# One-hot sort and eight queue-issued runs in place of indirect scatters, in a graph layer followed by a routed feed-forward layer

## The chip, the cores and the metric

One core of one Trainium2 chip runs the whole kernel. The metric is device time in microseconds (us) of one launch.

## The reference

For N = 12500 nodes with 256 features, 212500 edges sorted by destination, and 8 experts:

```python
# x: (12500, 256)   src, dst, edge_weight: (212500,)
msgs = layernorm(x)[src] * edge_weight[:, None]
x = x + (segment_sum(msgs, dst, 12500) @ W.T + b)          # graph layer
n = layernorm(x)
probs = softmax(n @ gate_w + gate_b)                       # 8 experts
top2_vals, top2_idx = top_k(probs, 2)
for e in range(8):                                         # routed layer
    w_e = top2_vals where top2_idx == e, else 0
    x = x + w_e[:, None] * (gelu(n @ W1[e] + b1[e]) @ W2[e] + b2[e])
```

## The kernel before

**Edges.** The edges stand in 208 groups of 1024. POOL fetches a group with 8 indirect gathers of 128 rows of 1 KB (L363). VectorE builds eight 128x80 spread matrices (L975), TensorE sums the group with 8 matmuls (L599), ScalarE copies the sums out (L782), TensorE turns them (L589) and VectorE adds them into a ring of node columns (L988). Three buffers of rows stand between POOL and TensorE.

**Nodes.** There are 98 tiles of 128 nodes. When a tile's groups are in, TensorE does the linear layer (L619), VectorE adds it to x and works out the layer norm (L1009 to L1025, `node`), ScalarE writes the normalised rows into `xs` (L788), and TensorE turns them (L630) and takes the gate's logits (L639). SP stores x1 (L475), which waits for VectorE's sum.

**Routing.** The tiles form 17 parts (6, then mostly 8, at the end 4 and 2 tiles). For a part, VectorE does the softmax, `choose` (the two largest, L1053 to L1073) and `place` (the row of each choice in its expert's queue, L1084 to L1141, with the list of items), with a count by TensorE between them (`rank`, L647 and L648). Then POOL sends each tile to the queues in DRAM with two indirect scatters of 128 rows of 1088 bytes (`send`, L391), one for the first choices and one for the second.

**Items.** 128 rows of one expert's queue are an item; there are 231. SP loads an item with an address read from a list (`load_xi`, L492 and L493). TensorE turns it (L655), multiplies by W1 (L667), turns the result (L676) after ScalarE's copy (L811), multiplies by W2 (L685) after ScalarE's gelu (L822). VectorE adds the bias and scales (L1152 to L1156), and POOL scatters the result rows (L396). VectorE's next but one item waits for that scatter to land. At the end of an epoch SP writes blank rows behind the eight queues (`fill_tails`, L480 and L481). Finally each node tile's two results are fetched and added to x1 (L504, L505, L1163, L1165) and stored (L510).

**Order.** All engines walk one list of turns that `plan` writes before the build. Turn t holds the gather of group t (POOL), the matmuls of group t-1, the turning of group t-2, at most one node tile, and one or two pipeline steps of items: in a step one item is at gelu and W2, the next at W1, a third is turned, and a fourth is loaded. So an item that SP loads in a turn with one step is turned by TensorE in the following turn. In 208 turns with gathers there is one step, or two in every other turn while over 6 items wait; after them come three steps a turn. Inside a turn TensorE's matmuls of the group come behind the first step, and a second step behind those. Each engine takes its instructions strictly in the order written; SP's order in a turn is:

```python
if t.load_x >= 0: load_x(t.load_x)
for step in t.steps:
    if step[3] >= 0: load_xi(step[3])
for u in t.combines: store_out(u)
for u in t.fetches: load_results(u, u in EPOCH_TILES)
if t.linear >= 0: store_x1(t.linear)
```

Of the kernel before, what the change touches and what calls it, by code (L numbers as in the profile page):

```python
# [35 lines left out]
RING = 16  # L36
# [23 lines left out]
NI = FIRST_ITEM[-1]  # L60
XI = 6
# [46 lines left out]
class Turn:  # L108
# [11 lines left out]
    sends: list = field(default_factory=list)  # L120
# [6 lines left out]
def plan(with_sums):  # L127
# [7 lines left out]
    while True:  # L135
# [87 lines left out]
def build(nc, x, src, dst, wgt_in, first, last, gnn_wT_in, gnn_b, gate_w, gate_b, w1_in, b1_in, w2_in, b2, out):  # L223
# [6 lines left out]
    xhat = nc.dram_tensor("xhat", (N, D), F32, kind="Internal").ap()  # L230
    blocks = slots.rearrange("(n p) f -> n p f", p=P)
    x_main, xhat_main = (a[0:P * LJ].rearrange("(p j) f -> p j f", p=P) for a in (x, xhat))
    with ExitStack() as s:
# [13 lines left out]
        iota_w, part_iota, valid = sb("iota_w", [P, W]), sb("part_iota", [P, 1]), sb("valid", [P, 1])  # L247
# [29 lines left out]
        top, top_r, slot_f = sb("top", [P, NTM]), sb("top_r", [P, NTM]), sb("slot_f", [P, NTM, 2])  # L277
        slot_i = sb("slot_i", [P, NT, 2], I32)
# [33 lines left out]
        sent, blank_out, tails_in = sems("sent", NK), sem("blank_out"), sem("tails_in")  # L312
# [26 lines left out]

        def wait_sent(eng, k):  # L340
            eng.wait_ge(sent[k], 32 * SIZES[k])
# [11 lines left out]
        def _(pool):  # L353
# [27 lines left out]
            nc.gpsimd.iota(block_f[0][:], pattern=[[BLOCKS, NX]], base=0, channel_multiplier=0, allow_small_or_imprecise_dtypes=True)  # L381
            nc.gpsimd.iota(item_iota[:], pattern=[[1, NI]], base=0, channel_multiplier=0,
# [3 lines left out]

            def send(t):
                k, n = PART_OF[t], valid_rows(t)
                pool.wait_ge(routed, k + 1)
                for c in range(2):  # L390
                    pool.indirect_dma_start(slots, bass.IndirectOffsetOnAxis(ap=slot_i[0:n, t, c:c + 1], axis=0),  # L391
                                            xs[0:n, t % XR, :], None).then_inc(sent[k], 16)
# [6 lines left out]
            def turns(plan, fast):  # L399
                for t in plan:  # L400
                    if t.gather >= 2:
                        if t.gather >= R:
                            pool.wait_ge(summed, t.gather - R + 1)
                        if t.gather == RAW:
                            wait_xhat()
                        gather(t.gather)
                    for u in t.sends:
                        send(u)
                    for i in t.results:
                        scatter_result(i)  # L410
# [17 lines left out]
        def _(sp):  # L428
# [41 lines left out]
            sp.wait_ge(blank_out, 16 * NX)  # L470
# [5 lines left out]

            def fill_tails(k):
                sp.wait_ge(routed, k + 1)
# [4 lines left out]
            def load_xi(i):  # L483
                k = part_of_item(i)
                if i == 0 or part_of_item(i - 1) != k:
                    sp.wait_ge(listed, k + 1)
                    wait_sent(sp, k)
# [34 lines left out]
            def turns(plan, fast):  # L522
                for t in plan:
                    if t.prep >= 0:
                        load_ahead(t.prep + 4)
                    if t.refill >= 0:
                        refill(t.refill)
                    if t.load_x >= 0:
# [12 lines left out]
                    if t.place >= 0 and ends_epoch(t.place):  # L541
                        fill_tails(t.place)
# [37 lines left out]
        def _(pe):  # L580
# [26 lines left out]
            def linear(t, fast):  # L607
# [8 lines left out]
                else:  # L616
                    pe.wait_ge(x1_ready, t)
                for k in range(KD):
                    done = nc.tensor.matmul(B_NODE[:, 0:D], tile(t)[:, k, :], gnn_wT[:, k, :], start=k == 0, stop=k == KD - 1)  # L619
                done.then_inc(lin_summed, 1)  # L620

# [79 lines left out]
            def turns(plan, fast):  # L701
                for t in plan:
                    for a, b, _, _ in t.steps[:1]:
                        step_up(a, b)
                    if t.add >= 0:
                        turn_sums(t.add)
                    if t.gate >= 0:
                        turn_node(t.gate)
                    if t.linear >= 0:
# [30 lines left out]
        def _(act):  # L740
# [43 lines left out]
            def normalise(t):  # L784
                if t >= XR:
                    wait_sent(act, PART_OF[t - XR])
                act.wait_ge(coef_ready, t + 1)
                nc.scalar.activation(xs[:, t % XR, 0:D], x_t[t % XB][:], ACT.Identity,  # L788
                                     bias=shift[t % XB][:], scale=rstd[t % XB][:]).then_inc(xn_ready, 1)

# [41 lines left out]
            def turns(plan, fast):  # L832
                for t in plan:
# [4 lines left out]
                    if t.prep >= 0:  # L838
                        block_root(t.prep)
                        normalise_rows(t.prep)  # L840
                    for a, b, _, _ in t.steps[:1]:
                        step_up(a, b)
                    if t.gate >= 0:
                        copy_xnT(t.gate)
                    for _, _, c, _ in t.steps[:1]:
                        if c >= 0:
                            copy_xiT(c)
                    if t.softmax >= 0:
# [23 lines left out]
        def _(dve):  # L872
            nc.vector.memset(eps[:], EPS)
            nc.vector.memset(acc[:], 0.0)
            nc.vector.memset(item_f[:], 0.0)
            for a in got + res:
# [35 lines left out]
            nc.vector.tensor_scalar(valid[:], part_iota[:], float(LAST), None, op0=ALU.is_lt)  # L912
            for n in keep_et:
                nc.vector.memset(keep_et[n][:, 0::n], 0.0)
            first_then(nc.vector.scalar_tensor_tensor(blank[:, C_ID:], id_base[:, 0:NX], float(2 * NPAD), blank[:, C_ID:],
                                                      op0=ALU.add, op1=ALU.add))
            nc.vector.memset(empty[:, 0:C_ID], 0.0)
# [158 lines left out]
            def place(k):  # L1076
# [10 lines left out]
                then(nc.vector.tensor_tensor(upto, upto, counts, op=ALU.subtract))  # L1087
                then(nc.vector.tensor_tensor(ps, by_expert(upto).rearrange("p e t -> p t e"), per_expert(end_old, n), op=ALU.add))
                nc.vector.tensor_tensor(ps, ps, B_GATE[:, 0:n * NX].rearrange("p (t e) -> p t e", e=NX), op=ALU.add).then_inc(gate_free, 1)
# [190 lines left out]
```

## Time and profile before

| | |
|---|---|
| time, median of 3 runs | 2976.65 us (2972.73 to 2977.03) |
| time of the profiled execution | 2972.42 us |
| its span, first to last instruction | 2970.7 us |
| granted TensorE clock, mean | 0.867 of full speed |
| busy: TensorE / VectorE / ScalarE / POOL | 74% / 47% / 25% / 68% |
| mean busy share of the 16 DMA engines | about 0.5, 146 GB/s |

SP does no arithmetic and has no row in the busy shares; what it does is read from the timeline of its queue. POOL's share counts only the body of each indirect DMA; the time between two of them is called "issue". In the rows, PE is TensorE, PEld its weight loads, DVE is VectorE, ACT is ScalarE, and SPq is SP's queue. A row's "<-" in brackets names what ended the idle time before it.

### The profile page before, as it was taken

How to read it: one execution, taken by the hardware profiler on the slowest of the kernel's cores; microseconds unless marked ns; L12 is line 12 of the kernel's file. 1: busy time of each engine (PE TensorE's matmuls, PEld its weight loads, DVE VectorE, ACT ScalarE, POOL GpSimd, SP SyncE). 2: the span in 40 equal slices, each digit the busy share in tenths (PEclk: the TensorE clock that was granted, in tenths of full speed). 3: DMA queues.
4: the chain of work that ended last, by engine and by line, in shares of the span. 5: the costliest groups of instructions: out<-in, count | busy, mean ns of one | idle time of the engine just before them, and what ended most of it. 6: DMA issues, size and time to landing. Idle time of an engine off the chain costs nothing.

```text
span 2970.7 us, 40845 instructions
## 1 busy us (share of the span) xinstructions
PE 2187.7 (74%) x9206; PEld 1475.6 (50%) x9207; DVE 1407.6 (47%) x5982; ACT 739.1 (25%) x1985; POOL 2011.7 (68%) x2107
## 2 busy tenths in 40 slices
PE   3555765785785978975966877977877887878655
PEld 2333543553563655653644654655555555545433
DVE  8756344344354444454463453453555455454342
ACT  3311110221221322220321221322222222224322
POOL 6547777777777777777777777777777777761211
PEclk9668877988898998987987987988998899889878
DMA  9563433443444443455555544434455565542352
GB/s 339 200 232 115 124 117 114 137 124 114 134 128 136 134 125 120 132 148 173 165 166 161 148 138 127 136 119 124 136 163 161 167 188 154 159 125 90 107 159 81
DMA packets 231445, 432.24 MB, mean 146 GB/s; under 512 B 47020, under 2 KB 158542, under 8 KB 228006
## 3 DMA queue, kind: packets, MB, share of 16 engines
q0 software_dynamic: 100368, 275.72, 31.2%
q1 hardware_dynamic: 128246, 144.38, 15.4%
q10 hardware_dynamic: 2592, 9.45, 0.8%
q8 instruction: 90, 1.47, 0.2%
q14 instruction: 149, 1.22, 0.1%
HBM read 326.80 MB, written 102.56 MB: 145 GB/s over the span
## 4 chain that ended last, share of the span: by engine, by line
POOL 51%; issue 19%; PE 14%; DVE 10%; DMA 3%; ACT 1%; ACTq 1%; DVEq 0%; SPq 0%; POOLq 0%
POOL rows L363 41%; POOL slots L391 5%; POOL results L396 5%; PE bank L599 5%; PE bank L685 4%; PE bank L667 3%; DVE spread L975 1%; DMA results<-y_sb,result_i 1%; PE bank L676 1%; DMA got<-results 1%; DVE item_t L1123 1%; DVE y_sb L1153 1%; DVE pre_bn L931 1%; DVE square_n L1022 0%; DVE bn L954 0%
## 5 line engine op out<-in xcount | busy, mean ns | idle before, releaser
L363 POOL DMA_INDIRECT rows<-xhat,src_t x1536 | 1469.2, 956 | 476.2 <-issue 464.7
L599 PE MATMUL bank<-rows,spread 128*80 128x256 f32 x3328 | 915.4, 437 | 317.1 <-issue 150.0
L599 PEld LDWEIGHTS bank<-rows,spread 128*80 128x80 f32 x3328 | 566.5, 176 | 603.9 <-issue 314.9
L685 PE MATMUL bank<-w,hT 128*128 x1848 | 482.6, 407 | 97.1 <-ACT hT L822 52.7
L685 PEld LDWEIGHTS bank<-w,hT 128*128 128x128 f32 x1848 | 361.4, 202 | 207.4 <-issue 160.9
L667 PE MATMUL bank<-w,xiT 128*128 x924 | 447.7, 607 | 12.5 <-ACT xiT L805 2.8
L988 DVE TENSOR_TENSOR acc<-acc,bank 128x160 f32 x208 | 67.0, 322 | 775.4 <-PE bank L589 753.0
L396 POOL DMA_INDIRECT results<-y_sb,result_i x231 | 227.2, 984 | 242.4 <-DVE y_sb L1156 186.3
L975 DVE TENSOR_SCALAR spread<-iota_w,dst_rel,wgt 128x80 f32<-128x80 f32 x1536 | 378.8, 342 | 0.2
L1152 DVE CAST result_i<-xi 128x1 int32 x231 | 35.5, 154 | 612.5 <-PE bank L685 327.8
L822 ACT ACTIVATE hT<-bank,b1T 128x128 f32<-128x128 f32 x924 | 263.3, 367 | 215.4 <-PE bank L676 209.6
L391 POOL DMA_INDIRECT slots<-xs,slot_i x196 | 190.7, 973 | 113.1 <-issue 79.0
L782 ACT ACTIVATE sums_n<-bank 80x256 f32<-80x256 f32 x192 | 71.2, 371 | 679.7 <-PE bank L599 679.7
L805 ACT ACTIVATE xiT<-bank 128x256 f32<-128x256 f32 x231 | 88.6, 383 | 579.5 <-PE bank L655 579.5
L667 PEld LDWEIGHTS bank<-w,xiT 128*128 128x128 f32 x924 | 159.4, 192 | 144.3 <-issue 143.7
L363 POOL DMA_INDIRECT rows<-in_x,src_t x128 | 122.3, 956 | 100.4 <-PE bank L603 60.4
L811 ACT ACTIVATE h_sb<-bank 128x512 f32<-128x512 f32 x231 | 138.7, 601 | 122.1 <-PE bank L667 122.0
L589 PEld LDWEIGHTS bank<-ident,sums_n 80*128 80x128 f32 x416 | 51.9, 144 | 224.9 <-ACT sums_n L782 138.7
L589 PE MATMUL bank<-ident,sums_n 80*128 80x80 f32 x416 | 69.8, 250 | 117.4 <-ACT sums_n L782 89.9
L788 ACT ACTIVATE xs<-x_t,shift,rstd 128x256 f32<-128x256 f32 x98 | 58.3, 595 | 351.7 <-DVE shift L1025 351.7
L676 PE MATMUL bank<-ident,h_sb 128*128 128x128 f32 x924 | 140.4, 275 | 1.9 <-ACT h_sb L811 1.9
L676 PEld LDWEIGHTS bank<-ident,h_sb 128*128 128x128 f32 x924 | 114.1, 143 | 23.8 <-ACT h_sb L811 2.8
(159 smaller groups left out, 1750.4 us busy)
## 6 DMA issues: line engine op xcount, KB each, us to landing
xi<-slots SPq DMA_DIRECT2D x231, 136.0 KB, 2.8
got<-results SPq DMA_DIRECT2D x97, 256.0 KB
rows<-xhat,src_t POOLq DMA_INDIRECT x1536
x_t<-in_x SPq DMA_DIRECT2D x97, 128.0 KB
x_d<-x_t SPq DMA_DIRECT2D x97, 128.0 KB, 2.4
res<-x_d SPq DMA_DIRECT2D x97, 128.0 KB
out_nodes<-res SPq DMA_DIRECT2D x97, 128.0 KB
w<-in_x SPq DMA_DIRECT2D x12, 1024.0 KB, 12.7
```

Source lines behind the costliest of these rows:

```text
L363: pool.indirect_dma_start(rows[q][:, c, :], None, x if g < RAW else xhat, bass.IndirectOffsetOnAxis(ap=src_t[:, g * CG + c:g * CG + c + 1] ...
L391: pool.indirect_dma_start(slots, bass.IndirectOffsetOnAxis(ap=slot_i[0:n, t, c:c + 1], axis=0), xs[0:n, t % XR, :], None).then_inc(sent[k] ...
L396: pool.indirect_dma_start(results, bass.IndirectOffsetOnAxis(ap=result_i[i % 2][:], axis=0), y_sb[i % 2][:], None).then_inc(y_out[i % 2], 16)
L589: done = nc.tensor.transpose(B_TURN[:, k * W:(k + 1) * W], sums_n[:, k * P:(k + 1) * P], ident[0:W, 0:W])
L599: done = nc.tensor.matmul(B_SUM[0:W, 0:D], spread[g % 2][:, c, :], rows[q][:, c, :], start=c == 0, stop=c == CG - 1)
L667: done = nc.tensor.matmul(B_H[:], xiT[i % 2][:, b, :], w1[:, bass.ds(e, 1), b, :].rearrange("p o h -> p (o h)"), start=b == 0, stop=b == K ...
L676: done = nc.tensor.transpose(B_HT[:, j * P:(j + 1) * P], h_sb[i % 2][:, j * P:(j + 1) * P], ident[:])
L685: done = nc.tensor.matmul(B_Y[:, 0:D], hT[i % 2][:, j, :], w2[:, bass.ds(e, 1), j, :].rearrange("p o f -> p (o f)"), start=j == 0, stop=j ...
L805: nc.scalar.activation(xiT[i % 2][:].rearrange("p k n -> p (k n)"), B_XI[:, 0:D], ACT.Copy).then_inc(xiT_ready, 1)
L811: nc.scalar.activation(h_sb[i % 2][:], B_H[:], ACT.Copy).then_inc(h_ready, 1)
L822: done = nc.scalar.activation(hT[i % 2][:, j, :], B_HT[:, j * P:(j + 1) * P], ACT.Gelu, bias=b1T[:, bass.ds(e * KH + j, 1)])
L975: done = nc.vector.tensor_scalar(spread[g % 2][:, c, :], iota_w[:], dst_rel[:, g * CG + c:g * CG + c + 1], w8[:, c:c + 1] if g < RAW else ...
```

## The change

POOL's `send` goes. In its place, one tile in each turn from the turn of its part's `place` on passes through four turns:

- `mask_choices` (VectorE, end of the turn): two 128x256 comparisons make a one-hot matrix. Its column is the place of a choice among the tile's 256 choices sorted by expert.
- `sort` (TensorE, next turn): two matmuls of that matrix with the tile's rows of `xs` (272 columns); ScalarE copies each result (`copy_sorted`). The bank is the one that `linear` uses, so `linear`, which now stands behind the first step, waits for the second copy.
- `store_sorted` (SP, the turn after): one store of the 256 sorted rows to one of three stage buffers in DRAM.
- `copy_runs` (SP, one turn later): for each of the 8 experts SP reads two registers (where the run starts in the stage, where it goes in the queue) and issues one DRAM to DRAM DMA of 128 rows. What lies behind the run's end is overwritten by the next tile's run, so each tile waits for all eight copies of the tile before.

`place` gets six more small instructions. The items of a part open only when the copies of its last tile have been issued, one tile a turn (before: two). After the last gather there is now one step a turn (before: three) until the last tile's copies are issued. The ring of node columns falls from 16 tiles to 8. In SP's turn the new work stands ahead of the loads of items:

```diff
@@ plan
-        for _ in range(2 if busy else 4):
-            if send_next < NT and place_at.get(PART_OF[send_next], tau) < tau:
-                t.sends.append(send_next)
-                if send_next == PARTS[PART_OF[send_next]][1] - 1:
-                    sent_at[PART_OF[send_next]] = tau
-                send_next += 1
+        if turns:
+            t.sort, t.stage, t.runs = turns[-1].mask, turns[-1].sort, turns[-1].stage
+        if send_next < NT and place_at.get(PART_OF[send_next], tau + 1) <= tau:
+            t.mask = send_next
+            send_next += 1
+        if t.runs >= 0 and t.runs == PARTS[PART_OF[t.runs]][1] - 1:
+            sent_at[PART_OF[t.runs]] = tau
-        n_steps = (1 + (waiting > 6 and tau % 2 == 0)) if busy else 3
+        n_steps = (1 + (waiting > 6 and tau % 2 == 0)) if busy else 1 if NK - 1 not in sent_at else 3
@@ SP
+            def store_sorted(t):
+                if t >= STAGES:
+                    sp.wait_ge(runs_in, 16 * NX * (t - STAGES + 1))
+                sp.wait_ge(sorted_ready, 2 * t + 2)
+                sp.dma_start(stages[t % STAGES][0:2 * P].rearrange("(h p) f -> p h f", p=P), sorted_x[t % 2][:]).then_inc(staged[t % STAGES], 16)
+            def copy_runs(t):
+                k = PART_OF[t]
+                j = (t - PARTS[k][0]) * NX
+                sp.wait_ge(routed, k + 1)
+                sp.wait_ge(staged[t % STAGES], 16 * (t // STAGES + 1))
+                if t:
+                    sp.wait_ge(runs_in, 16 * NX * t)
+                if t in EPOCH_TILES[1:]:
+                    sp.wait_ge(tails_in, 16 * NX * EPOCH_OF[k])
+                for e in range(NX):
+                    a = sp.value_load(run_from[k % 2][:, j + e:j + e + 1], min_val=0, max_val=2 * P)
+                    b = sp.value_load(run_to[k % 2][:, j + e:j + e + 1], min_val=0, max_val=NX * S - 2 * P)
+                    sp.dma_start(slots[bass.ds(b, P), :], stages[t % STAGES][bass.ds(a, P), :]).then_inc(runs_in, 16)
@@ SP turns
                     if t.refill >= 0:
                         refill(t.refill)
+                    if t.stage >= 0:
+                        store_sorted(t.stage)
+                    if t.runs >= 0:
+                        copy_runs(t.runs)
                     if t.load_x >= 0:
                         load_x(t.load_x)
@@ TensorE
                     if t.add >= 0:
                         turn_sums(t.add)
+                    if t.sort >= 0:
+                        sort(t.sort, 0)
                     if t.gate >= 0:
                         turn_node(t.gate)
+                    for a, _, c, _ in t.steps[:1]:
+                        step_down(a, c)
+                    if t.sort >= 0:
+                        sort(t.sort, 1)
                     if t.linear >= 0:
                         linear(t.linear, fast)
-                    for a, _, c, _ in t.steps[:1]:
-                        step_down(a, c)
@@ VectorE
+            def mask_choices(t):
+                nc.vector.tensor_scalar(first_choice[:], iota_s[:], at[0], None, op0=ALU.is_equal).then_inc(half_mask, 1)
+                nc.vector.scalar_tensor_tensor(sort_mask[t % 2][:], iota_s[:], at[1], first_choice[:],
+                                               op0=ALU.is_equal, op1=ALU.add).then_inc(mask_set, 1)
```

## Rows read from the trace of the kernel before

**Rows 1.** The page's chain that ended last, by engine and line.

```profile
POOL 51%; issue 19%; PE 14%; DVE 10%; DMA 3%; ACT 1%; ACTq 1%; DVEq 0%; SPq 0%; POOLq 0%
```

**Rows 2.** Busy time by engine from 256 to 2676 us, with instruction counts.

```profile
256.00:2676.00 2420.00, 1851.41 (x7781) 1250.00 (x7781) 1126.91 (x4755) 571.00 (x1550) 1813.37 (x1886) 0.88 0.47 140
```

**Rows 3.** Timeline of POOL at 1283 us: start, duration.

```profile
1285.04 0.97 POOL L363 DMA_INDIRECT rows<-xhat,src_t  x1 [0.30 <-issue]
...
1295.07 0.99 POOL L396 DMA_INDIRECT results<-y_sb,result_i  x1 [0.30 <-issue]
```

**Rows 4.** Timeline of TensorE: group sums that bound the long stage.

```profile
250.85 5.34 PE L599 MATMUL bank<-rows,spread 128*80 128x256 f32 x16 [1.14 <-issue]
...
1062.61 3.65 PE L599 MATMUL bank<-rows,spread 128*80 128x256 f32 x16
...
1285.26 3.68 PE L599 MATMUL bank<-rows,spread 128*80 128x256 f32 x16 [0.73 <-DMA rows<-xhat,src_t]
...
2670.26 5.79 PE L599 MATMUL bank<-rows,spread 128*80 128x256 f32 x16
...
2680.77 3.65 PE L599 MATMUL bank<-rows,spread 128*80 128x256 f32 x16 [0.34 <-issue]
```

**Rows 5.** Timeline of TensorE: first instructions of two turns, and of the second's extra step.

```profile
1219.63 0.60 PE L676 MATMUL bank<-ident,h_sb 128*128 128x128 f32 x4
...
1229.15 0.60 PE L676 MATMUL bank<-ident,h_sb 128*128 128x128 f32 x4
...
1233.25 0.60 PE L676 MATMUL bank<-ident,h_sb 128*128 128x128 f32 x4
```

**Rows 6.** Waits between 1066 and 1289 us: total us, times, longest.

```profile
DVE result_i L1152 <- DMA results<-y_sb,result_i: 29.2, 6, 9.1
```

**Rows 7.** Waits between 500 and 2600 us: total us, times, longest.

```profile
PEld bank L599 <- DMA rows<-xhat,src_t: 112.1, 24, 10.0
...
PEld bank L647 <- DVE both L1067: 84.1, 12, 12.7
```

**Rows 8.** SP's instructions for a blank store with an address: duration ns min/median/max.

```profile
L480 SPq TENSOR_LOAD <-end_i x40: 263/273/524, 893.3 to 2841.9; - x40
L480 SPq FUSED_REGOPS  x40: 147/147/154, 893.6 to 2842.2; - x40
L480 SPq SEQ_ASSERT  x40: 18/18/18, 893.7 to 2842.4; - x40
...
L481 SPq FUSED_REGOPS  x40: 42/42/42, 893.8 to 2842.5; - x40
L481 SPq MOVE slots<-blank x40: 29/29/37, 893.9 to 2842.6; - x40
L481 SPq DMA_DIRECT2D slots<-blank x40: 332/332/761, 894.0 to 2842.6; - x40
```

**Rows 9.** Timeline of SP's queue at 2834 us.

```profile
2834.73 8.21 SPq L481 DMA_DIRECT2D slots<-blank  x8
```

**Rows 10.** Timeline of SP's queue at 1501 us.

```profile
1502.87 0.43 SPq L510 DMA_DIRECT2D out_nodes<-res  x1
1503.40 0.37 SPq L504 DMA_DIRECT2D res<-x_d  x1
1503.82 0.48 SPq L505 DMA_DIRECT2D got<-results  x1
```

**Rows 11.** DMA issues by line: KB each, median us to landing.

```profile
xi<-slots SPq DMA_DIRECT2D x231, 136.0 KB, 2.8
...
slots<-blank SPq DMA_DIRECT2D x40, 136.0 KB, 2.5
```

**Rows 12.** Groups by line: busy us, mean ns of one.

```profile
L805 ACT ACTIVATE xiT<-bank 128x256 f32<-128x256 f32 x231 | 88.6, 383 | 579.5 <-PE bank L655 579.5
```

**Rows 13.** Timeline of TensorE in the tail: two items' first steps, and the last item.

```profile
2861.80 0.60 PE L676 MATMUL bank<-ident,h_sb 128*128 128x128 f32 x4
...
2866.28 0.60 PE L676 MATMUL bank<-ident,h_sb 128*128 128x128 f32 x4
...
2939.91 1.99 PE L685 MATMUL bank<-w,hT 128*128 x8 [1.41 <-ACT hT L822]
```

**Rows 14.** The page's DMA queues: packets, MB, share of 16 engines.

```profile
q0 software_dynamic: 100368, 275.72, 31.2%
q1 hardware_dynamic: 128246, 144.38, 15.4%
```

More of the change, by code:

```diff
@@ L35 @@
 NPAD = NT * P
-RING = 16
+RING = 8
 RCOLS = RING * P
@@ L60 @@
 NI = FIRST_ITEM[-1]
+STAGE = 3 * P
+STAGES = 3
 XI = 6
@@ L119 @@
     refill: int = -1
-    sends: list = field(default_factory=list)
+    mask: int = -1
+    sort: int = -1
+    stage: int = -1
+    runs: int = -1
     steps: list = field(default_factory=list)
@@ L230, in build @@
     xhat = nc.dram_tensor("xhat", (N, D), F32, kind="Internal").ap()
+    stages = [nc.dram_tensor(f"stage{i}", (STAGE, XW), F32, kind="Internal").ap() for i in range(STAGES)]
     blocks = slots.rearrange("(n p) f -> n p f", p=P)
@@ L469, in _ @@
                 sp.dma_start(blocks[(e + 1) * BLOCKS - 1], empty[:]).then_inc(blank_out, 16)
-            sp.wait_ge(blank_out, 16 * NX)
+            for a in stages:
+                sp.dma_start(a[2 * P:], blank[:]).then_inc(blank_out, 16)
+            sp.wait_ge(blank_out, 16 * (NX + STAGES))
             def store_x1(t):
@@ L527, in turns @@
                         refill(t.refill)
+                    if t.stage >= 0:
+                        store_sorted(t.stage)
+                    if t.runs >= 0:
+                        copy_runs(t.runs)
+                        k = PART_OF[t.runs]
+                        if t.runs == PARTS[k][1] - 1 and ends_epoch(k):
+                            fill_tails(k)
                     if t.load_x >= 0:
@@ L620, in linear, with sort @@
                 done.then_inc(lin_summed, 1)
+            def sort(t, h):
+                if h == 0:
+                    pe.wait_ge(mask_set, t + 1)
+                pe.wait_ge(x1_ready, n_linear[0])
+                if t or h:
+                    pe.wait_ge(sorted_ready, 2 * t + h)
+                nc.tensor.matmul(B_NODE[:, 0:XW], sort_mask[t % 2][:, h * P:(h + 1) * P], xs[:, t % XR, :],
+                                 start=True, stop=True).then_inc(sort_done, 1)
+            n_linear, n_sorted = [0], [0]
             def turn_node(t):
@@ L847, in turns @@
                             copy_xiT(c)
+                    if t.sort >= 0:
+                        copy_sorted(t.sort, 1)
                     if t.softmax >= 0:
@@ L875, in _ @@
             nc.vector.memset(item_f[:], 0.0)
+            nc.vector.memset(xs[:], 0.0)
+            nc.vector.memset(keep_te[:], 1.0)
             for a in got + res:
@@ L916, in _ @@
                                                       op0=ALU.add, op1=ALU.add))
+            nc.vector.memset(keep_te[:, 0::NX], 0.0)
             nc.vector.memset(empty[:, 0:C_ID], 0.0)
@@ L1096, in place @@
                         dve.wait_ge(tails_in, 16 * NX * EPOCH_OF[k])
-                    nc.vector.tensor_copy(end_i[:], end[0:1, :])
-                nc.vector.tensor_copy(slot_i[:, t0:t1, :], slot_f[:, 0:n, :]).then_inc(routed, 1)
+                    then(nc.vector.tensor_copy(end_i[:], end[0:1, :]))
+                dve.sem_inc(routed, 1)
                 if ends_epoch(k):
-                    dve.wait_ge(routed, k + 1)
                     then(nc.vector.tensor_scalar(round_i[:], end[:], float(P - 1), None, op0=ALU.add))
@@ L1104, in place @@
                 list_items(k, end)
+            def mask_choices(t):
+                k = PART_OF[t]
+                j = t - PARTS[k][0]
+                at = [place_f[k % 2][:, c, j:j + 1] for c in range(2)]
+                if t:
+                    dve.wait_ge(mask_set, t)
+                if t >= 2:
+                    dve.wait_ge(sort_done, 2 * (t - 2) + 2)
+                nc.vector.tensor_scalar(first_choice[:], iota_s[:], at[0], None, op0=ALU.is_equal).then_inc(half_mask, 1)
+                dve.wait_ge(half_mask, t + 1)
+                nc.vector.scalar_tensor_tensor(sort_mask[t % 2][:], iota_s[:], at[1], first_choice[:],
+                                               op0=ALU.is_equal, op1=ALU.add).then_inc(mask_set, 1)
             def list_items(k, end):
```

68 lines of the change are left out of this document (46 added, 22 removed).

## The prediction

> **What bounds the kernel now.** I read the page's chain first: POOL's indirect DMAs and the issue time between them are 70% of it [rows 1]. The busy table of the long stage, 256 to 2676 us, says how full POOL is: 1886 instructions in 2420 us [rows 2], one each 1.28 us, while POOL's timeline has them 10.03 us / 8 = 1.254 us apart when nothing is waited for [rows 3]. So POOL is 98% full there. The page's 68% hides this, since it leaves out the 0.30 us before each.
>
> The second thing is how near TensorE is. From the end of group 16's sums (256.2) to that of group 206 (2676.1) there are 190 turns of 12.74 us [rows 4]. In POOL's own terms: 1520 gathers, 184 scatters of tiles and 188 of results, by the planner's rules, 1892 x 1.254 = 2373 us. TensorE waited for rows only 112 us in 2100 [rows 7]. One part of 17 turns, groups 85 to 101, took 1288.9 - 1066.3 = 222.7 us [rows 4], of which 29.2 us were VectorE waiting for POOL's result scatters [rows 6]. Without POOL it would have been 193.5 us, 11.4 a turn. This is what TensorE's chain adds up to: 17 x 9.5 us for a turn with one step, 6 x 4.1 us for second steps [rows 5], and 84.1 / 12 = 7.0 us in the turn of `choose`, where the count and then the group's sums stand behind VectorE [rows 7]: 193.1 us. So TensorE's chain is only 1.3 us a turn below POOL.
>
> SP is the engine to look at, since the work goes there. It is idle most of a turn, but strictly in order, and an item that it loads in one turn is turned in the next.
>
> **The change, part by part.**
>
> *POOL.* 184 scatters go in the long stage and 6 result scatters move past it: 190 x 1.254 = 238 us. POOL then needs 1702 x 1.254 = 2134 us, 11.2 a turn. This is the most that the long stage can gain, and only if all else keeps that pace.
>
> *TensorE, ScalarE, VectorE.* A sort is two matmuls of 272 columns. Eight of 256 columns take 3.65 us [rows 4], so 2 x 0.46 x 1.06 = 0.97 us, and where `linear` follows it waits for ScalarE's second copy, 0.38 us [rows 12] and a hand-over: 1.4 us a tile. It can't be below nothing, and if both copies are waited for it is some 2. `linear` behind the first step moves the node's norm, `choose` and the count later by a W2 product and a turn, 1.9 + 0.4 = 2.3 us, in 14 turns. The masks (two comparisons of 256 columns, some 0.9 us) and `place`'s six instructions (some 1.3 us) lie in VectorE's idle half, and in the rest between `place` and the next spread. If that cover is gone they cost 8 x 0.9 + 1.3 us a part.
>
> *SP.* This decides. A blank store with one address from a register has a period of (8.21 - 0.33) / 7 = 1.13 us [rows 9]. Its pieces are the load, its range arithmetic and assertion, 0.273 + 0.147 + 0.018 = 0.44 us, the address, 0.07 us, and the DMA, 0.33 us, with some 0.05 us between any two of the six [rows 8]. No row shows a DMA with two addresses from registers. From below: the second costs nothing, 1.13 us. From above: a second load with its gaps, 0.58, a second address, 0.17, and the slowest DMA issue seen, 0.76 for 0.33 [rows 8]: 2.3 us. I take 1.13 + 0.58 + 0.17 = 1.88, rounded to 1.85 us, since the second load is the same work as the first. Eight are 14.8 us a tile.
> The Trainium skill (DMA: Bandwidth & Descriptors, Latency and other measured facts) gives a floor of about 600 ns for a tensor load. The row has 0.27 us. By the page's figure a run would be an estimated 2.5 us, a tile 20, and the kernel near 3600 us; the row decides.
>
> The rest of SP's turn with runs: the store of the sorted rows 0.5, 63 items over 90 such turns at 1.13, 0.8; x and x1, 0.4; results in 32 of them at some 1.45 [rows 10], 0.5; semaphore waits 0.2. That is 2.4, and 17.2 us together, against TensorE's 11 to 12.
>
> Who waits: behind the copies in SP's queue stands the load of the item that TensorE turns in the next turn. At the first turn with copies SP has most of a turn in hand; from the second on TensorE gets its item at SP's pace, 17.2 us a turn, and with TensorE wait the group's sums, and so POOL's rows. By the planner's rules 90 turns of the 190 have copies, in 14 bursts (6, seven of 8, then 8, 6, 4, 4, 4 and two of the last 4). 90 - 14 = 76 turns go at SP's pace: 76 x 17.2 = 1307 us. In 23 of the 90 no item is loaded, and SP can be a turn further behind before two full buffers of sorted rows stop ScalarE: back 50 us.
>
> The other 114 turns go at TensorE's pace, since POOL has three buffers in hand after a burst: 102 x 9.5, 12 without a step x 5.4, 38 second steps x 4.1, 14 x (7.0 + 2.3) for `choose`, 42 sorts x 1.4: 969 + 65 + 156 + 130 + 59 = 1379 us. POOL needs 1280 for them.
>
> The long stage: 1307 - 50 + 1379 = 2636 for 2420 us, +216.
>
> *Tail.* Before, it is 2970.7 - 2684.4 = 286 us [rows 4]. After: turns 209 to 222 hold 7 turns with copies at some 18 us (two fetches of results each), less 4 x 6 in hand, and 7 at some 8 us, 158 us. Then items 197 to 230, 34 x 4.48 us [rows 13], 152, less 13 that lie in turn 222, and as before 29 us from the last product to the end [rows 13]: 326, +40 us. The idle stretch of the old tail is filled, but by slow turns. Start (a memset, three more blanks) and twelve folds for six: +8 us.
>
> Sum, on the profiled execution's own 2972.4 us, which is 4.2 below the median of the runs and is kept as the base: 2972.4 + 216 + 40 + 8 = 3236; I say 3240 us.
>
> **The rivals.**
>
> *The copies are cheap or hidden: faster.* If a run cost 1.13 us, SP's turn would be 11.5 us and never late. TensorE's chain would then bound, 193.5 + 8 x 1.4 + 2.3 = 207 us a part, 12.2 a turn: -105 us, with a tail of some 280: about 2865 us, and by POOL alone 2690. For it: DMA issue alone is 0.33 of the 1.13 us [rows 8]. Against it: the rest is there each time, and now twice. It decides from SP turns of 13.7 us down, a run of 1.4 us.
> The Trainium skill (Perfetto Trace Analysis, What "DMA-bound" means) names solid DMA slices on the issuing engine's track as the sign that the issuer binds, and large descriptors as the help. By that rule alone the eight large copies are 3 us of slices and this rival holds; the register loads between the slices are not in it.
>
> *Part of it is hidden.* Runs of 1.45 to 1.65 us, or SP further ahead at each burst than I think: 2985 to 3130 us.
>
> *The copies themselves are slow.* A tile now moves 8 x 128 rows from DRAM to DRAM. At the SP queue's mean of 0.154 x 16 x 2970.7 / 128246 = 57 ns a packet that is 3.7 us of all 16 DMA engines, at the indirect queue's 148 ns it is 9.5 us [rows 14], with some 8 us a turn of other traffic [rows 2]. Landing is 2.5 to 2.8 us for such a size [rows 11], and each tile waits for the eight before, issued last some 2.5 us earlier: little or no wait. If they land in 6 us, each turn grows by 3.5: 76 x 3.5 = 266, some 3500 us.
>
> *No change*: needs the gain on POOL and the loss on SP to meet within 6 us.
>
> **How the numbers follow.** SP's pace as costed, 3130 to 3360 us: 0.60. Slow copies or issue, above that: 0.10. Part hidden: 0.11. Within 0.2% (about what a measurement of this kernel can tell from no change): 0.03. Faster: 0.16. Slower is 0.60 + 0.10 + 0.11 = 0.81. The range is 2985 to 3440 us: it leaves out the faster and the equal case and the far end of the slow ones, some 2 in 10.
>
> **What would show it.** SP's queue in a burst: rows of eight copies some 1.85 us apart, and hardly idle. TensorE in those turns waits for the load of xi, 5 us a turn, which today costs it next to nothing. POOL is no longer full: it waits for the sums of a group. Turns are 17 us in bursts and 10 to 13 between. It would be wrong if the copies stand 1.4 us apart or less, if POOL's issues stay 1.25 us apart through the stage, or if TensorE's waits for xi stay small.

## The result, and the profile after

The changed kernel takes 3613.71 us (3610.18 to 3620.73), beside 2976.84 us for the kernel before on the same chip: ratio 1.215, interval 1.2134 to 1.2165, 637 us more. The forecast was 3240 us with a range of 2985 to 3440: the direction was right, the loss was 2.4 times the one forecast. The profiled execution took 3620.73 us (span 3619.0, mean clock 0.82), and the rows of after are from it.

The chain, by engine and by line, to be set against [rows 1]:

```profile
SPq 36%; PE 25%; DVE 15%; issue 13%; DMA 7%; ACT 1%; ACTq 1%; POOL 0%; DVEq 0%; POOLq 0%
SPq L501 13%; SPq L500 10%; SPq L499 10%; PE bank L630 8%; PE bank L712 6%; PE bank L730 6%; DMA slots<-stage 4%; DVE spread L1041 2%; PE bank L721 1%; DMA xi<-slots 1%; PE bank L662 1%; DVE item_t L1214 1%; PE bank L700 1%; DVE square_n L1088 1%; DMA got<-results 1%
```

In the chain, SP had 0% and has 36% now. 33% are three lines: the two register loads (L499, L500) and the copy (L501). POOL fell from 51% to 0%.

Busy time of the long stage, which now runs from 239 to 3212 us ([rows 2]):

```profile
239.00:3212.00 2973.00, 1971.86 (x8042) 1333.97 (x8043) 1201.13 (x4989) 636.89 (x1699) 1630.87 (x1696) 0.82 0.50 147
```

POOL has 190 instructions fewer, as costed, but the stage is 553 us longer. The DMA share is 0.50 beside 0.47: on the mean the transfers don't fill the 16 DMA engines. TensorE's granted clock fell from 0.88 to 0.82 in this stage, where it waits more. That isn't where the time went: without the sort's matmuls (L662, 142 us) TensorE was busy for 1830 us, beside 1851 before, with six items fewer in the stage.

SP's queue in a burst (start, duration; [rows 9, 10]):

```profile
310.34 14.53 SPq L501 DMA_DIRECT2D slots<-stage  x8
324.96 0.52 SPq L466 DMA_DIRECT2D x_t<-in_x  x1
325.57 0.38 SPq L486 DMA_DIRECT2D stage<-sorted_x  x1
329.28 14.48 SPq L501 DMA_DIRECT2D slots<-stage  x8
```

From one block of eight copies to the next it is 18.94 us here, in a turn that loads no item and no results. The pieces of a run are in the instruction rows ([rows 8]; duration ns min/median/max):

```profile
L499 SPq TENSOR_LOAD <-run_from x784: 262/271/901, 290.6 to 3430.7; - x196
L499 SPq FUSED_REGOPS  x784: 147/147/159, 291.1 to 3431.3; - x196
L499 SPq SEQ_ASSERT  x784: 18/18/31, 291.3 to 3431.5; - x196
```

```profile
L501 SPq MOVE slots<-stage x1568: 29/29/43, 292.2 to 3432.3; - x196
L501 SPq FUSED_REGOPS  x784: 60/60/66, 292.1 to 3432.2; - x196
L501 SPq DMA_DIRECT2D slots<-stage x784: 525/531/717, 292.4 to 3432.4; - x196
```

The load and its arithmetic cost what the blank store's did, and come twice. The issue of a DRAM to DRAM copy with two register addresses takes 0.531 us where the blank store's took 0.332.

Waits over the whole run (total us, times, longest; [rows 7]):

```profile
PE bank L700 <- DMA xi<-slots: 622.9, 62, 42.5
```

```profile
POOL rows L374 <- PE bank L630: 506.8, 63, 35.8
```

```profile
SPq L495 <- DMA slots<-stage: 34.2, 32, 2.0
```

TensorE waits for the load of an item, and POOL for TensorE. SP stands idle for the copies' landing (L495 is `copy_runs`' wait) for 34 us in all. The chain's 4% for the landing are more, some 145 us, since the chain counts the whole time from the issue of a block's last copy to its landing; in most of that time SP issues other transfers, and only the rest is idle. One such piece of the chain, beside the SP rows above (start, duration):

```profile
324.33 3.07 DMA slots<-stage
```

SP issued until 325.95 and then idled until 327.41. Two rows of TensorE's timeline show that bursts in which no item is loaded are late too:

```profile
330.12 1.25 PE L662 MATMUL bank<-xs,sort_mask 128*128 128x272 f32 x2 [9.87 <-ACT sorted_x L846]
...
403.26 0.69 PE L700 MATMUL bank<-ident,xi 128*128 128x128 f32 x2 [42.54 <-DMA xi<-slots]
```

In the first the sort waits for ScalarE, whose two buffers of sorted rows wait for SP's store. In the second the first item behind a burst pays SP's whole lag at once.

### The profile page after: what moved, and what is told of

Same layout as the page of the kernel before. It is cut to its first block, busy times and chain, and to the rows that moved or that the text cites. A ratio compares the mean times of both kernels' runs of the same rounds, so it can differ in the third digit from the quotient of the medians.

```text
span 3619.0 us, 50501 instructions
## 1 busy us (share of the span) xinstructions
PE 2351.8 (65%) x9598; PEld 1586.3 (44%) x9599; DVE 1495.4 (41%) x6264; ACT 822.3 (23%) x2181; POOL 1823.7 (50%) x1912
## 3 DMA queue, kind: packets, MB, share of 16 engines
q8 instruction: 94, 1.54, 0.2%
## 4 chain that ended last, share of the span: by engine, by line
SPq 36%; PE 25%; DVE 15%; issue 13%; DMA 7%; ACT 1%; ACTq 1%; POOL 0%; DVEq 0%; POOLq 0%
SPq L501 13%; SPq L500 10%; SPq L499 10%; PE bank L630 8%; PE bank L712 6%; PE bank L730 6%; DMA slots<-stage 4%; DVE spread L1041 2%; PE bank L721 1%; DMA xi<-slots 1%; PE bank L662 1%; DVE item_t L1214 1%; PE bank L700 1%; DVE square_n L1088 1%; DMA got<-results 1%
## 5 line engine op out<-in xcount | busy, mean ns | idle before, releaser
L700 PE MATMUL bank<-ident,xi 128*128 128x128 f32 x462 | 106.1, 317 | 622.9 <-DMA xi<-slots 622.9
L712 PE MATMUL bank<-w,xiT 128*128 x924 | 474.6, 639 | 10.4 <-ACT xiT L862 2.2
L700 PEld LDWEIGHTS bank<-ident,xi 128*128 128x128 f32 x462 | 66.4, 159 | 667.6 <-DMA xi<-slots 648.0
L662 PE MATMUL bank<-xs,sort_mask 128*128 128x272 f32 x392 | 151.2, 472 | 202.9 <-DVE sort_mask L1194 161.7
L712 PEld LDWEIGHTS bank<-w,xiT 128*128 128x128 f32 x924 | 168.3, 203 | 152.3 <-issue 151.0
L662 PEld LDWEIGHTS bank<-xs,sort_mask 128*128 128x128 f32 x392 | 70.1, 221 | 215.1 <-DVE sort_mask L1194 167.6
```

The costliest lines, as they stand in the source:

```text
L662: nc.tensor.matmul(B_NODE[:, 0:XW], sort_mask[t % 2][:, h * P:(h + 1) * P], xs[:, t % XR, :], start=True, stop=True).then_inc(sort_done, 1)
L700: done = nc.tensor.transpose(B_XI[:, b * P:(b + 1) * P], xi[i % XI][:, b * P:(b + 1) * P], ident[:])
L712: done = nc.tensor.matmul(B_H[:], xiT[i % 2][:, b, :], w1[:, bass.ds(e, 1), b, :].rearrange("p o h -> p (o h)"), start=b == 0, stop=b == K ...
```

## The experiments

Eighteen runs were made. Twelve had chips where the kernel before took 2973 to 2978 us. Six (e5 to e8, e17, e18) had chips where it took 3706 and 3713 us; their ratios stand only beside each other. The microseconds of the two kinds are not compared. The edits are shown shortened. In the expectations, theory A is that SP's instructions set the pace, theory B that it is the sort, the masks, the order or the tail plan, theory C that it is the copies' transfers or their landing.

| run | us | over the kernel before on its chip | ratio, interval |
|---|---|---|---|
| e1_pool_scatters | 3137.94 | +165 | 1.055 (1.0519 to 1.0581) |
| e2_third_load | 4066.56 | +1094 | 1.3672 (1.3630 to 1.3714) |
| e3_double_bytes | 3723.45 | +750 | 1.2518 (1.2482 to 1.2555) |
| e4_items_first | 3653.65 | +681 | 1.2284 (1.2248 to 1.2319) |
| e9_changed_again | 3625.86 | +651 | 1.2176 (1.2146 to 1.2206) |
| e10_one_load | 3276.77 | +302 | 1.1009 (1.0975 to 1.1043) |
| e11_spread | 3124.79 | +150 | 1.0507 (1.0490 to 1.0525) |
| e12_combined | 2964.05 | -11 | 0.9963 (0.9950 to 0.9976) |
| e13_spread_mask_first | 3109.66 | +132 | 1.0455 (1.0435 to 1.0476) |
| e14_spread_one_load | 3002.03 | +24 | 1.0087 (1.0071 to 1.0104) |
| e15_tail_three_steps | 3619.86 | +642 | 1.2162 (1.2133 to 1.2191) |
| e16_scatters_mask_first | 3150.32 | +172 | 1.0587 (1.0569 to 1.0605) |
| e5, one load | 4188.22 | +483 | 1.1295 (1.1262 to 1.1329) |
| e6, spread | 4158.49 | +453 | 1.1210 (1.1164 to 1.1255) |
| e7 and e18, split | 4310.95, 4325.39 | +605, +612 | 1.1640, 1.1604 |
| e8, combined | 3884.99 | +179 | 1.0499 (1.0464 to 1.0534) |
| e17_copies_last | 4472.13 | +759 | 1.2030 (1.1991 to 1.2069) |

**e1: without the copies.** Masks, sort, stage store and order stay; POOL sends each tile by two scatters in place of SP's copies.

```diff
-                        copy_runs(t.runs)          # SP
+                        send(t.runs)               # POOL, two indirect scatters
```

> The changed kernel with its plan, masks, sort, ScalarE copies and store of the sorted rows, but the rows go to the queues by POOL's two indirect scatters a tile in the turn where SP copied the runs; SP's copies are gone (the sorted rows are stored and not used; place has some five more small instructions). Theory A (SP's in-order copies, 19 us a tile, are what is lost): near the kernel before plus the sort and the later items, 2980 to 3080 us. Theory B (the sort on TensorE, the masks behind place, the later linear and the tail plan are what is lost): 3300 us or more. Theory C (the traffic from DRAM to DRAM): as A.

3138 us: SP's copies in place of POOL's scatters are 476 of the 637 us. (That is the exchange of the two, since POOL has its scatters back in this run; `place` has some five more small instructions.) The other 165 (stage 2563 for 2420 us, tail 327 for 286, start 17 us sooner) belong to sort, masks, `place`, the smaller ring of node columns and the new order; the ring was in no run changed by itself. TensorE's waits for the loads of items, 623 us in the changed kernel, are gone with the copies:

```profile
PE bank L694 <- DMA xi<-slots: 4.3, 2, 3.7
```

**e2: one register load more per run.**

```diff
                     b = sp.value_load(run_to[k % 2][:, j + e:j + e + 1], ...)
+                    sp.value_load(run_to[k % 2][:, j + e:j + e + 1], ...)
```

> The changed kernel with one more register load per run, whose value is not used: 8 x 0.56 = 4.5 us more of SP a tile. Theory A: every tile's copies lie on the path, so 98 x 4.5 = 440 us more, about 4050 us. Theory B: SP is not what sets the pace, under 60 us more. Theory C (the copies' transfers set the pace): the loads lie beside them, under 100 us more.

+453 us, 98 x 4.6: a run's pace is 2.480 us for 1.915. A register load with its arithmetic, 0.565 us on SP, moves no byte of the payload and costs its full length, in every tile.

**e3: twice the rows in each copy.** Nothing is left out; the rows beyond a run are overwritten as before.

```diff
-                    sp.dma_start(slots[bass.ds(b, P), :], stages[t % STAGES][bass.ds(a, P), :])
+                    sp.dma_start(slots[bass.ds(b, 2 * P), :], stages[t % STAGES][bass.ds(a, 2 * P), :])
```

> The changed kernel with copies of 256 rows for 128 (stages of 512 rows): twice the bytes from DRAM to DRAM, the same number of instructions on SP. Theory A: no change to speak of, 3600 to 3660 us. Theory C (transfer or landing of the copies sets the pace): 200 us more at least. Theory B: no change.

+110 us for 109 MB more. A run's pace stays (1.913 us for 1.915); SP's wait for the landing grew:

```profile
SPq L496 <- DMA slots<-stage: 127.7, 68, 4.2
```

That is 94 us more, most of the 110. So the transfers have a price, a small one at the changed kernel's size.

**e4: all of SP's new work behind the item, x and result loads.**

```diff
+                    [load_x, load_xi, store_out, load_results]
                     if t.stage >= 0:
                         store_sorted(t.stage)
                     if t.runs >= 0:
                         copy_runs(t.runs)
-                    [load_x, load_xi, store_out, load_results]
```

> The changed kernel with the store of sorted rows and the copies moved behind the loads of items, x and results in SP's turn. Theory A: the item that TensorE waits for is loaded some 16 us earlier, but SP still needs 19 us a tile, so each of the 14 long bursts gains at most one block: 14 x 16 = 220 us less, 3370 to 3450 us. Theory B and C: under 60 us.

A miss: 40 us slower instead of 160 to 240 faster. The items' loads stand in front, and TensorE waits for them nearly as long as before (593 us for 623); the stage's store went back with the copies, and ScalarE now waits for it, for 246 us, where it was 40:

```profile
PE bank L700 <- DMA xi<-slots: 593.2, 51, 53.6
```

```profile
ACT sorted_x L846 <- DMA stage<-sorted_x: 246.0, 35, 15.9
```

So SP is short of time, and not only badly ordered; the reading that what stands first in its turn is late because the turn before was too long fits these waits, and e17 below tries it with the store left in front.

**e5 and e10: one load per run.** Both addresses are packed into one 32-bit number by VectorE, and SP takes them apart with register arithmetic.

```diff
-                    a = sp.value_load(run_from[...])
-                    b = sp.value_load(run_to[...])
+                    both_at = sp.value_load(run_from[...])
+                    a, b = both_at >> 17, both_at & ((1 << 17) - 1)
```

> Start and target of each run are packed into one 32-bit number, so that a run needs one register load in place of two (a shift and a mask of registers come in). Theory A (SP's instructions set the pace, 19.0 us a turn and 4.6 us a block for one load with its arithmetic, as the third load cost): 8 x (0.56 - about 0.15) = 3.3 us off each of 98 blocks, so 320 us less than the changed kernel: 3230 to 3340 us. Theory B (sort, masks and order set the turns): no change beyond 30 us, 3580 to 3620. Theory C (the transfers themselves): no change either.

> The changed kernel as it is, beside the next three on one chip: in the four runs before these the kernel before took 3706 us instead of 2973, on another chip, so their times can't be set against 3614. If this chip is like the first: 3600 to 3630. If it is like the other: some 4400, and the differences to the next three count.

> One register load per run instead of two, as in the earlier run of this edit. In undisturbed stretches of that run a run's pace was 1.455 us against 1.915 with two loads, 3.7 us a block. Theory A: 90 blocks at SP's pace and 8 in the tail: 98 x 3.7 = 360 less than the changed kernel, 3240 to 3300 us on a chip like the first. Theory B or C: within 30 of the changed kernel.

e5 has no 2973 us beside it and isn't compared in microseconds. e9 is the changed kernel again; e10 against it on one chip: -349 us. A run's pace is 1.454 us for 1.915, from block to block 15.3 us for 19.1:

```profile
304.09 11.32 SPq L502 DMA_DIRECT2D slots<-stage  x8
315.51 0.53 SPq L466 DMA_DIRECT2D x_t<-in_x  x1
316.13 0.39 SPq L486 DMA_DIRECT2D stage<-sorted_x  x1
318.74 10.71 SPq L502 DMA_DIRECT2D slots<-stage  x8
```

With the same bytes and the same plan this rules out transfers, sort and order as the cause of these 349 us. The sort's wait for its mask stayed at 162 us, TensorE's for items fell from 628 (e9) to 351.

**e6 and e11: blocks of copies in every second turn** while sums run, through the masks. 58 items instead of 47 are left for the tail.

```diff
         if send_next < NT and place_at.get(PART_OF[send_next], tau + 1) <= tau \
+                and not (busy and turns[-1].mask >= 0):
```

> While sums run, a tile's masks are made in every second turn only, so that blocks of eight copies come in every second turn (8 adjacent pairs of turns with copies instead of 81). Nothing is left out; 58 items instead of 47 are left for the turns after the last sums. Theory A: SP has 19 us of work per two turns, TensorE 24 or more, so the copies fall off the path: the stage goes from 2973 to near that of the POOL scatters (2563), and 11 more items behind it cost some 50: 3170 to 3260 us. A total below 3138 would say that the copies, once hidden, are cheaper than POOL's scatters. Theory B or C: over 3500.

> Copies in every second turn while sums run. Theory A: the copies fall off the path, the stage comes near 2563 as with POOL's scatters, 11 more items behind it cost some 50: 3170 to 3260 us on a chip like the first. Theory B or C: over 3500.

e11 took 501 us less than e9, 45 below the fastest time expected. The stage takes 2358 us, 205 less than e1's and 62 less than the kernel before. The tail rose to 512 us, for 399 in the changed kernel and 327 in e1. So not all of the 205 are POOL's relief, forecast as 238 at the most: 11 items and three tiles' copies left the stage for the tail, at 4.48 us an item [rows 13] some 50 us. In total e11 is only 13 us below e1.

**e13, e14, e8 and e12: what the rest is worth.** e13 is the spread with a part's first mask ahead of its list of items, e14 the spread with one load; e8 and e12 are one kernel with both and three item steps a turn in the tail.

```diff
+                if mask >= 0:
+                    mask_choices(mask)      # inside place
                 list_items(k, end)
```

> Copies in every second turn and a part's first mask ahead of its list of items; two loads a run, the changed kernel's tail plan. If the waits of TensorE's sort for sort_mask (162 us in 21 turns of the changed kernel, 14 parts, some 8 to 11 us each) are on the path: 80 to 130 less than e11_spread, 2995 to 3045. If they only stand where another wait would: within 20 of 3125.

> Copies in every second turn and one load per run. SP still has 8 adjacent pairs of turns with copies, and its later loads (item, results) come 3.7 us sooner in each turn with copies: if these loads are waited for, 20 to 70 less than e11_spread, 3055 to 3105; the tail's 15 blocks alone give 15 x 3.7 = 55 at most.

> Together: one load per run, copies in every second turn, three item steps a turn in the tail as before, and the first mask of a part ahead of the list of items (TensorE's sort waited 162 us for sort_mask in 21 turns behind it). Theory A plus the cure of the mask's place: spread's time, less some 100 for the masks, less 20 to 40 for the tail: 3020 to 3130 us. Faster than the kernel before (2973) would need the sort's own 1.4 us a tile to be paid by POOL's lighter load.

> One load per run, copies in every second turn, three item steps a turn in the tail, a part's first mask ahead of its list of items. Theory A: 3020 to 3130 us on a chip like the first, below e11_spread by 100 or more; a tie with e11_spread would say that neither the loads nor the mask's place nor the tail plan cost anything once the copies have room.

Against e11 the mask's place gives 15 us (forecast 80 to 130, a miss), one load 123 (forecast 20 to 70, low), all together 161. Of the 123, 75 lie in the stage, which takes 2283 us in e14 (and in e12 as well), and 43 in the tail, 469 us for 512:

```profile
239.00:2522.00 2283.00, 1820.64 (x7824) 1230.50 (x7824) 1190.25 (x4962) 605.13 (x1622) 1618.48 (x1685) 0.91 0.63 186
```

So what e12 has over e14, 35 us by the kernel before on each one's chip, lies in the tail alone (433 for 469 us); the mask's place, 3 us of stage in e13, adds nothing to the stage there. The waits for the mask did fall, 151 to 70 us in e13, and those of the sums for instruction issue rose from 81 to 142: the wait moved. e12 at 2964.05 us is 0.4% faster than the kernel before, with an interval of the ratio that stays below 1. Its stage, chain and two waits:

```profile
239.00:2522.00 2283.00, 1825.94 (x7827) 1234.35 (x7827) 1196.75 (x4962) 604.87 (x1623) 1621.45 (x1685) 0.91 0.64 187
```

```profile
PE 28%; POOL 26%; issue 17%; DVE 12%; SPq 10%; DMA 5%; ACT 1%; ACTq 1%; DVEq 0%; POOLq 0%
```

```profile
PE bank L701 <- DMA xi<-slots: 71.3, 16, 16.7
...
PE bank L663 <- DVE sort_mask L1199: 33.7, 8, 15.2
```

137 us are won in the stage, and the tail gives back 147 (433 for 286 us), since 58 items are turned there by TensorE (before: 41) and the copies of the last 11 tiles stand there; the start gives 17. SP still has 10% of the chain.

**e15: the tail plan alone.**

```diff
-        n_steps = (...) if busy else 1 if NK - 1 not in sent_at else 3
+        n_steps = (...) if busy else 3
```

> The changed kernel with up to three item steps in every turn behind the last sums, as before, 236 turns instead of 239. The prediction put the tail at +40 us, most of it waits of the last items for SP: 0 to 40 less than the changed kernel's 3614 to 3626. Theory A (SP sets the pace in the tail too): within 15 of it.

3619.86 us, tail 398 for 399: no effect here. The steps allowed don't matter where SP brings the items too late; with one load a run and more items left, e12's tail was 36 us shorter than e14's.

**e16: e1 with e12's mask place and tail plan.**

> e1_pool_scatters (POOL's scatters in place of SP's copies, sort kept, 3138 us) with the mask's place and the tail plan of e12_combined. If the mask's wait and the tail made its 165 us over the kernel before: 2990 to 3040. If the sort's own work (1.4 us for each of 98 tiles, and the later linear) made it: 3090 or more.

3150 us, 12 over e1: the mask's wait and the tail plan don't make e1's 165. The mask's wait fell from 177 to 62 us here as well, and little came of it: the stage is 7 us shorter, the tail 17 longer. That leaves the sort's own work, the later `linear`, and what else e1 keeps (`place`'s instructions, the smaller ring, the later opening of items); for each of them only this exclusion speaks. (Copies last together with e12's edits wasn't tried.)

**e17: only the copies last, the stage's store in its place.**

> Only copy_runs and fill_tails go behind the loads of items, x and results; the stage's store stays in front, other than in e4. If SP's total in a turn sets the pace (19.0 us, theory A): within 40 of the changed kernel, since only a burst's first turns differ. If it is the place of the item's load behind the copies: 200 or more less, below 3420 us.

The store is in front here, and yet TensorE waits for items and ScalarE for the stage's store, as in e4 (on a slower chip, so the sizes aren't compared):

```profile
PE bank L700 <- DMA xi<-slots: 849.6, 50, 70.2
```

```profile
ACT sorted_x L846 <- DMA stage<-sorted_x: 311.1, 26, 18.7
```

So the store's place can't be the whole reason for e4's miss.

**e7 and e18: runs 4 to 7 on ScalarE's queue.**

```diff
+                    if t.runs >= 0:                # ScalarE, ahead of its copies
+                        copy_runs(t.runs)          # runs 4 to 7; SP keeps 0 to 3
```

> Runs 4 to 7 of each tile go through ScalarE's DMA queue, with the same waits, runs 0 to 3 stay with SP; the same bytes, the same turns. Theory A: SP's turn falls from 19.0 to about 11 us and ScalarE's rises by about 8 from 4 or 5, both under TensorE's 12.6; stage 2600 to 2750, total 3200 to 3370 us. Theory C (landing of copies, contention): over 3500, as the bytes and the times between blocks stay. Theory B: over 3500. If ScalarE's waits for the staged tile hold up its copies for TensorE, somewhere between.

> Runs 4 to 7 of a tile on ScalarE's queue, runs 0 to 3 on SP's. Theory A: SP's turn falls to about 11 us, and ScalarE gets 8 us of issue more in each turn with runs, which now stand ahead of its copies for TensorE and wait for the stage's store to land: 3200 to 3400 us. Theory C (landing, contention): over 3550. ScalarE's queue as a new bound of its own would show as TensorE's waits for sorted_x and for xiT instead of for xi.

e7, e17 and e18 had the slower chips, without the changed kernel beside them, so neither question is settled in microseconds. e17's waits, and its ratio of 1.203 beside 1.13 for one load on such a chip, speak for SP's total in a turn again, but the ratio of the changed kernel there isn't known. By the ratios, split is better than e17 and worse than one load (e5). Its trace (e7) names the new bound: ScalarE's queue is as strictly in order as SP's, and its sorted copies now stand behind waits for copies to land:

```profile
ACT sorted_x L861 <- DMA slots<-stage: 504.7, 40, 17.4
```

```profile
PE bank L662 <- ACT sorted_x L861: 653.4, 62, 17.3
```

## Why the prediction was wrong

The mechanism was right: SP's eight runs set the pace in bursts, and TensorE waits for xi there. The number failed mainly in two steps, both on SP's side: the credit for slack and the length of SP's turn. Over the 81 pairs of successive blocks the mean pace, from the first load of one block to that of the next, is 19.0 us. If all 90 turns with copies in the stage are counted at the block pace, the rest of the stage comes out within 17 us of the same in five kernels with the same plan:

| | block pace | 90 x pace | stage | the other 100 turns |
|---|---|---|---|---|
| after | 19.02 | 1712 | 2973 | 1261 |
| e2 | 23.57 | 2121 | 3379 | 1258 |
| e3 | 20.12 | 1811 | 3069 | 1258 |
| e10 | 15.30 | 1377 | 2652 | 1275 |
| e15 | 19.12 | 1721 | 2979 | 1258 |

Read the other way, the stage changes against the changed kernel's by 89 times the change of the pace in e2, 87 times in e3 and 86 times in e10, not by 76.

- **"76 turns go at SP's pace", "back 50 us": failed, 148 us.** All 90 do, or nearly. That a burst's first turn has SP's slack in hand, and that turns without an item let SP fall behind, would only help if the lag were never called in. The next item calls it in (the 42.54 us row), and ScalarE's two buffers before that (9.87 us). 14 x (19.0 - 12) is 98, and the credit was 50. Its count was off as well: by the plan 23 of the 90 turns have no pipeline step, and 38 load no item, so there was even more slack of this kind, and it gave nothing.
- **"17.2 together": 19.0, 137 us over 76 turns.** The run was costed at 1.85 us and has a pace of 1.915 (median) and 1.953 (mean): 0.8 us a block. The parts: two loads as costed, the second address cheaper, and an issue of 0.53 us instead of 0.33. The upper bound had a slow issue in it, the value taken had not. The remaining 1.0 us is the rest of SP's turn. Some of it can be read from the trace: the two loads of a block's first run took 0.95 us together where 0.54 were costed (the row of L499 has up to 0.90 for one), and SP idled 0.42 us a pair for the landing alone (34.2 us over 81 pairs), where the sum had 0.2 for all waits. The other 0.4 us weren't worked out.
- **"The other 114 turns": 52 us.** At 19.0 us a block 1263 us are left for 100 turns, 12.6 each, where the sum gives 1379 - 14 x 12 = 1211, 12.1 each. The sort's wait for its mask behind `place` and the list of items was left out of it, 162 us in the whole run; e13 and e16 say that its removal gives 15 us or nothing in their kernels, so it isn't the cause by itself. The sort was costed too low: its matmuls kept TensorE busy for 142 us in the stage, 1.54 us for each of 92 tiles where the sum had 0.97, and that is 16 us for the 28 sorts in these 100 turns. What the rest of the 52 us is stays open.
- **The tail, +40: +113.** Three parts of it are measured: with POOL's scatters it is 327 us (+41), the copies add 72, the step plan nothing. The sum had taken 4 x 6 us in hand and 7 turns at 18 us. Of the five pairs of successive blocks there, three have the 18 to 19 us costed and two 21 to 22 (next rows, one of the two), and some 6 to 9 turns follow SP's pace (440 us with a third load, 375 with one). So the slack taken in hand fails here too, by the same argument as in the stage; how the 72 us divide wasn't worked out.

```profile
3317.94 14.33 SPq L501 DMA_DIRECT2D slots<-stage  x8
...
3338.91 6.25 SPq L501 DMA_DIRECT2D slots<-stage  x4
```

- **The start, +8: -17.** The stage begins at 239.0 us instead of 256.2. Which of the edits does it wasn't tried.

The terms add up by construction, since each is measured less forecast: 148 + 137 + 52 + 73 - 25 = 385, and 3236 + 385 = 3621, the profiled time.

- **POOL, 238 us as a possible gain: not refuted.** e11's stage is 205 us below e1's, and some 50 of these are items moved to the tail.
- **Sort and the later `linear`, 1.4 us a tile and 2.3 a part:** some 150 us in all, beside e1's +143 in the stage. The sizes agree, but the matmuls took longer than costed (1.54 us for 0.97), and e1 has POOL near its limit too, so the agreement doesn't prove the split.
- **Rival "cheap or hidden": wrong as the change stands, and right about what is needed.** Its point of decision was an SP turn of 13.7 us. e10 at 15.3 us is still slower; in e14 and e12 a block comes every 22.7 and 23.1 us, for two turns, and they come to within 1% and below. The Trainium skill's rule on solid slices (Perfetto Trace Analysis, What "DMA-bound" means) would have called this the winner. The trace doesn't agree: the copies' own slices are 0.53 of 1.915 us, and the 1.1 us of loads and arithmetic between them decided.
- **Rival "copies slow", 3500 us: near the time, not the cause.** Its place was the landing, for which SP idled 34 us, and twice the bytes cost 110 us (e3). The Trainium skill's floor for a tensor load (DMA: Bandwidth & Descriptors, Latency and other measured facts), with which the sum came to about 3600 us, is near by accident too: the loads took 0.27 us, as the row of before had said.

## What to carry to other kernels

When work moves to a queue that runs strictly in order, cost the whole turn of that queue, and give no credit for slack: here the bursts cost the queue's pace for 86 to 90 of 90 turns, since something later waited for the lag each time. A copy with its addresses in registers cost its register loads and their arithmetic, over half a microsecond each, before any byte moved: pack what the loads bring, and spread the blocks over the turns that have room. The same edit lost 637 us and, with one load a run and blocks in every second turn, came to within 24 us of the old kernel, and 11 us below it with the mask's place and the tail plan; that last step lies in the tail.

## What the runs showed of the hardware

- Issuing a DRAM to DRAM copy of 128 rows (landed as before) with two addresses from registers occupied SP for 0.531 us; a blank store with one address 0.332 us. Which of the two differences makes it wasn't tried.
- 109 MB more through SP's queue cost 110 us in a kernel of 3614 us (e3).
- On two chips the kernel before took 3706 and 3713 us. There one in ten of SP's MOVEs for the copies (158 of 1568 in e5) took over 0.4 us in place of 0.03, most of them 0.6 to 0.9 and one 1.6; the median stayed. In e10 none did. The rows of e5 (first) and of e10 (second), the same kernel:

```profile
L502 SPq MOVE slots<-stage x1568: 1/29/1587, 313.5 to 4003.3; - x196
```

```profile
L502 SPq MOVE slots<-stage x1568: 14/29/101, 289.0 to 3081.7; - x196
```

The "issue" share of the chain was 29% there beside 13%. Other engines show it too, but not POOL: ScalarE idled 194 us before its copies of items (`xiT`) without a wait that the profile shows, beside 5 us in e10, POOL 466 us before its gathers, beside 491. Why, no run shows. The edits that keep SP's copies lose more there against the kernel before: the ratio is 1.050 instead of 0.996 for the combined kernel, 1.130 instead of 1.101 for one load.
